# Low parts of x before the second norm, POOL for weight and constant splits, roots and scans in PSUM, and both projections on split parts

## The chip, the core and the metric
The kernel runs on one core of one Trainium2 chip. TensorE (PE) multiplies matrices into PSUM; VectorE (DVE), ScalarE (ACT) and GpSimd (POOL) work on tiles of 128 partitions; SyncE (SP) issues DMAs. Each engine works through its own queue in order, and semaphores tie the queues together. The metric is the device time of one execution in microseconds.

## The reference
The input x is 2 sequences of 512 tokens of 256 channels in float32. It is normalised, and the result xn goes through a gated linear recurrence and a ternary feed-forward network; both results are added to x:

```python
xn = layernorm(x)                                   # eps 1e-5, no scale
y = gelu(xn @ w_y + b_y)                            # exact gelu
xb = xn @ w_x + b_x
conv = conv_b + sum(conv_w[k] * shift(xb, 3 - k) for k in range(4))   # causal, per channel
gate_x, gate_a = sigmoid(conv @ w_ig + b_ig), sigmoid(conv @ w_ag + b_ag)
a = exp(-8 * gate_a * softplus(a_param));  mult = sqrt(1 - a * a)
a, mult = 0, 1 at t == 0
h[t] = a[t] * h[t-1] + gate_x[t] * conv[t] * mult[t]
attn = (h * y) @ w_out + b_out
q(w) = clip(round(w / mean|w|), -1, 1) * mean|w|    # hidden size 682
ffn = (silu(xn @ q(w1).T) * (xn @ q(w3).T)) @ q(w2).T
out = x + attn + ffn
```

## The kernel before, in words
Channels lie on partitions (2 chunks `c` of 128) and tokens along the free dimension, 512 for each sequence `s`. Nothing is scheduled by a planner: each engine has one hand-written list of steps, and the calls at its end set its order.

**Split products.** For a float32 product at the speed of fp32r matmuls a value is split into `hi` (a copy rounded to fp32r, mostly by ScalarE) and `lo` (value minus `hi`, by POOL or VectorE). A product is then three matmuls: w_hi with v_hi, w_lo with v_hi, w_hi with v_lo. The ternary weights are exact and need no low part. Only the projection with w_out (L706) multiplies plain float32.

**Stages.** TensorE keeps itself busy with products of ones (`warm`, L713). VectorE takes mean and variance of each token tile (L436, L441), POOL the root (L231, `pow`), VectorE normalises (L449). TensorE transposes (L636), ScalarE writes `xt_hi` (L288), VectorE `xt_lo` (L455). The product with w_x of sequence 0 (L740) works by halves of the sequence; `dense_terms` (L647) does all other products of the recurrent part. The newest tap of the convolution comes from ScalarE (L317), a correction of its first 3 columns (L488) and three older taps (L492) from VectorE. The gates follow (tanh, exp), then `squares` (a*a, L526). Ten tiles `n` = (s, j) of the hidden layer (L664) each pass through ScalarE's silu (L332), VectorE's product `g_of` (L514), ScalarE's `g_hi` (L338) and POOL's `g_lo` (L256); `silu` and `g` are rings of 3. A tail of 42 hidden units is handled by L673, L558, L566, L567 and L572. `down` (L696) sums the feed-forward output in PSUM.

**The end.** ScalarE takes four roots (`mult_of`, L370) after a table load. VectorE does for each of the four pairs (s, c) `gated_products` (L533), `scan` (L538) and `gated_output` (L544), all in SBUF, in place in `tx`. `project` adds w_out's product onto the same PSUM banks. VectorE adds x (L551), SP stores five pieces (L208).

## Time and profile before
| | |
|---|---|
| times of three runs | 75.23, 75.66, 76.0 us; median 75.66 |
| the profiled execution | 75.99 us, span 74.2 |
| granted TensorE clock | 1.0 of full speed |
| PE busy | 69.2 us, 93% of the span |
| DVE busy | 61.2 us, 82% |
| ACT busy | 48.3 us, 65% |
| POOL busy | 31.5 us, 43% |
| chain that ended last | PE 80%, DMA 7%, DVE 5%, SP's queue 3% |

Busy time of PE is that of matmuls that overlap, so it doesn't say that PE works at its peak. The chain is followed back from the last instruction to what released each one, so it shows where a saved microsecond counts. A row of the timeline gives the start, the duration, the engine and line, the tiles out<-in with their shapes, how many instructions are merged in it, and in brackets the idle time before it with what ended it. The duration of a row of several overlapping instructions is from the first start to the last end.

### The profile page before, as it was taken

The page shows a single profiled execution, that of the slowest core. Times are in us where ns is not written, and L with a number is a line of the kernel's source. Part 1 is how long each engine was busy: PE and PEld are TensorE (multiplying, and loading weights), DVE is VectorE, ACT ScalarE, POOL GpSimd, SP SyncE. Part 2 cuts the span into 40 slices and gives each one's busy share as a digit, 9 for nine tenths or more (in the row PEclk, how much of TensorE's full clock was granted, in tenths as well). Part 3 has the DMA queues.
Part 4 walks back from the last instruction along what each step waited for, and adds up shares of the span by engine and source line. Part 5 has one row for each costly group of instructions (what it writes and reads, how often), then busy time and mean ns, then how long its engine had stood idle before and what let it go on. Part 6 is the DMA issues. An engine that isn't in the chain of part 4 may idle for free.

```text
span 74.2 us, 1064 instructions
## 1 busy us (share of the span) xinstructions
PE 69.2 (93%) x364; PEld 58.6 (79%) x364; DVE 61.2 (82%) x101; ACT 48.3 (65%) x75; POOL 31.5 (43%) x43
## 2 busy tenths in 40 slices
PE   4999969999999999999999999999999999999920
PEld 4985758877888888888888888888899999988800
DVE  4897499999999999999979974697960799999750
ACT  3674523899999999999998978466699910000000
POOL 6385647245851680016002979947689000000000
PEclk9999999999999999999999999999999999999999
DMA  0889999920000000000000000000000000000195
GB/s 8 236 289 333 368 379 342 379 97 9 0 0 0 4 0 0 0 0 0 4 1 0 0 9 0 0 0 0 0 0 0 0 0 0 9 0 0 61 322 183
DMA packets 5095, 5.63 MB, mean 76 GB/s; under 512 B 525, under 2 KB 4578, under 8 KB 5090
## 3 DMA queue, kind: packets, MB, share of 16 engines
q1 hardware_dynamic: 4946, 5.55, 22.1%
q8 instruction: 3, 0.05, 0.3%
...
## 4 chain that ended last, share of the span: by engine, by line
PE 80%; DMA 7%; DVE 5%; SPq 3%; issue 1%; DVEq 0%
PE slot L664 25%; PE slot L647 23%; PE slot L696 14%; PE slot L706 8%; DMA x_sb<-x 7%; PE slot L767 4%; PE slot L673 2%; SPq L186 2%; DVE stats L436 2%; PE slot L740 2%; DVE x_sb L551 1%; PE slot L636 1%; DVE xt_lo L455 1%; SPq L183 1%; DVEq L52 0%
## 5 line engine op out<-in xcount | busy, mean ns | idle before, releaser
L256 POOL TENSOR_TENSOR g_lo<-w_raw,g_hi 128x512 fp32r<-128x512 f32 x10 | 14.1, 1421 | 9.0 <-ACT g_hi L338 8.9
L664 PE MATMUL slot<-xt_hi,w_q 128*128 128x512 f32 x40 | 15.7, 393 | 0.0
L664 PE MATMUL slot<-xt_lo,w_q 128*128 128x512 f32 x40 | 15.7, 393 | 0.0
L514 DVE SCALAR_TENSOR_TENSOR w_raw<-w_raw,s,slot 128x512 f32<-128x512 f32 x10 | 7.3, 747 | 3.1 <-ACT w_raw L332 3.0
L696 PE MATMUL slot<-w_q,g_hi 128*128 128x256 f32 x40 | 9.7, 283 | 0.0
L696 PE MATMUL slot<-w_q,g_lo 128*128 128x256 f32 x40 | 9.7, 283 | 0.0
L492 DVE SCALAR_TENSOR_TENSOR conv<-slot,par,conv 128x511 f32<-128x511 f32 (+2 forms) x12 | 9.0, 748 | 0.4
L664 PEld LDWEIGHTS slot<-xt_hi,w_q 128*128 128x128 f32 x40 | 7.5, 188 | 1.7
L664 PEld LDWEIGHTS slot<-xt_lo,w_q 128*128 128x128 f32 x40 | 7.5, 188 | 1.7
L332 ACT ACTIVATE w_raw<-slot,scale 128x512 f32<-128x512 f32 x10 | 6.6, 684 | 3.1 <-PE slot L664 3.1
L696 PEld LDWEIGHTS slot<-w_q,g_lo 128*128 128x128 f32 x40 | 7.7, 192 | 0.0
L696 PEld LDWEIGHTS slot<-w_q,g_hi 128*128 128x128 f32 x40 | 7.7, 192 | 0.0
L226 POOL TENSOR_TENSOR w_lo<-w_raw,w_hi 128x512 fp32r<-128x512 f32 x4 | 5.2, 1295 | 4.5 <-ACT w_hi L283 3.7
L706 PE MATMUL slot<-w_raw,tx 128*128 128x256 f32 x32 | 7.1, 379 | 0.0
L338 ACT ACTIVATE g_hi<-w_raw 128x512 fp32r<-128x512 f32 x10 | 6.3, 629 | 1.1 <-DVE w_raw L514 0.9
L251 POOL TENSOR_TENSOR conv_lo<-conv,conv_hi 128x512 fp32r<-128x512 f32 x4 | 5.4, 1354 | 3.3 <-ACT conv_hi L342 3.3
L706 PEld LDWEIGHTS slot<-w_raw,tx 128*128 128x128 f32 x32 | 6.0, 190 | 0.8
L713 PE MATMUL slot<-ones 128*128 128x128 f32 x28 | 5.3, 357 | 1.0 <-POOL ones L214 1.0
L713 PEld LDWEIGHTS slot<-ones 128*128 128x128 f32 x28 | 4.8, 261 | 1.4 <-POOL ones L214 1.0
L533 DVE TENSOR_TENSOR tx<-tx,mult 128x512 f32<-128x512 f32 x4 | 2.7, 685 | 2.8 <-ACT mult L370 2.8
L538 DVE TENSOR_TENSOR_SCAN tx<-ta,tx 128x512 f32<-128x512 f32 x4 | 4.9, 1224 | 0.1
L647 PE MATMUL slot<-conv_hi,w_hi 128*128 128x512 f32 x12 | 4.7, 395 | 0.0
...
## 6 DMA issues: line engine op xcount, KB each, us to landing
...
```

The lines of the kernel that those rows point to most:

```text
L226: nc.gpsimd.tensor_tensor(w_lo[:, m], w_raw[:, m], w_hi[:, m].bitcast(f32), ALU.subtract).then_inc(w_lo_set, 1)
L251: nc.gpsimd.tensor_tensor(conv_lo[:, s, c], conv[:, s, c], conv_hi[:, s, c].bitcast(f32), ALU.subtract).then_inc(conv_lo_set, 1)
L256: nc.gpsimd.tensor_tensor(g_lo[:, j, s], g[:, n % RING], g_hi[:, j, s].bitcast(f32), ALU.subtract).then_inc(g_lo_set, 1)
L332: nc.scalar.activation(silu[:, n % RING], slot[H_SLOT[s][j]][:, 0], ACT.Silu, scale=scale[:, 0:1]).then_inc(silu_set, 1)
L338: nc.scalar.activation(g_hi[:, j, s], g[:, n % RING], ACT.Copy).then_inc(g_hi_set, 1)
L492: nc.vector.scalar_tensor_tensor(out=conv[:, s, c, i:], in0=slot[X_SLOT[s]][:, c, 0:SEQ - i], scalar=par[:, CONV_W + KC * k + c:CONV_W + K ...
L514: nc.vector.scalar_tensor_tensor(out=g[:, n % RING], in0=silu[:, n % RING], scalar=s32[:, 0:1], in1=slot[H_SLOT[s][j]][:, 1], op0=ALU.mult ...
L647: mm = nc.tensor.matmul(dst[:, o], w[:, m, c, o * P:(o + 1) * P], v[:, c], start=(first and i == 0 and c == 0), stop=(last and i == len(te ...
L664: mm = nc.tensor.matmul(slot[H_SLOT[s][j]][:, o], w13_q[:, c, col:col + P], v[:, s, c], start=(c == 0 and v is xt_hi), stop=(c == KC - 1 a ...
L696: nc.tensor.matmul(out_tile(s, i, t), v[:, s, rows], w2_q[:, j], start=(j == 0 and t == tiles.start and k == 0), stop=False, skip_group_ch ...
L706: mm = nc.tensor.matmul(out_tile(s, i, t), tx[:, s, c, t * P:(t + 1) * P], w_raw[:, WOUT, c], start=False, stop=(c == KC - 1), skip_group_ ...
L713: nc.tensor.matmul(slot[WARM_SLOT][:, 0, 0:P], ones[:, :], ones[:, :], start=True, stop=True)
```

## The change
1. The low parts of x of sequence 0 come before the statistics of sequence 1 on VectorE, whose x is now loaded, measured and normalised in halves. TensorE does the product of half 0 with low parts before half 1.
2. POOL adds eps (L444 is gone), forms the constants of the taps behind the roots, makes w_hi of WIG, WAG and WOUT (a copy, `CAST`), w_lo of WY in two chunks behind the second norm, the decay rates, the padding of `gt` and the last `g_hi`.
3. The first 3 columns of the convolution are no longer corrected: `first_columns` writes them from PSUM with their own constants.
4. A gelu of one column early on ScalarE brings its table load forward.
5. The last silu stands behind g_hi(8). Roots are written to PSUM (`state`), in three banks that the hidden layer has left, and product and scan work there in place.
6. `gated_output` still writes `tx`. ScalarE copies it to `hy_hi`, POOL subtracts to `hy_lo` (the memory of `conv_hi` and `conv_lo`), and `project` uses three fp32r matmuls where there was one in float32. The fourth store is issued by ScalarE.

```diff
...
+        hy_hi, hy_lo = conv_hi, conv_lo
...
+        S_BANK = (slot[1][:, 1], slot[2][:, 0], slot[2][:, 1])
+        def state(s, c):
+            return S_BANK[(KC * s + c) % len(S_BANK)]
...
-            sp.dma_start(x_sb[:, 1], x_dram[1]).then_inc(x_loaded[TILES], 16)
+            for i in range(2):
+                t = slice(i * TILES // 2, (i + 1) * TILES // 2)
+                sp.dma_start(x_sb[:, 1, t], x_dram[1][:, t]).then_inc(x_loaded[TILES + i], 16)
...
-            for n, (s, i) in enumerate(O_ALL):
-                sp.wait_ge(o_set, n + 1)
-                t = slice(O_TILES[s][i].start, O_TILES[s][i].stop)
-                sp.dma_start(out_dram[s][:, t], x_sb[:, s, t]).then_inc(out_stored, 16)
+            for n in (0, 1, 2, 4):
+                store(sp, n)
...
+            def square_hi(m):
+                pool.wait_ge(w_loaded[m], 16)
+                nc.gpsimd.tensor_copy(w_hi[:, m], w_raw[:, m]).then_inc(w_hi_set, 1)
+            def square_lo(m, chunks=range(KC)):
                 pool.wait_ge(w_hi_set, m + 1)
-                nc.gpsimd.tensor_tensor(w_lo[:, m], w_raw[:, m], w_hi[:, m].bitcast(f32), ALU.subtract).then_inc(w_lo_set, 1)
+                c = slice(chunks.start, chunks.stop)
+                nc.gpsimd.tensor_tensor(w_lo[:, m, c], w_raw[:, m, c], w_hi[:, m, c].bitcast(f32), ALU.subtract).then_inc(w_lo_set, len(chunks))
...
+                pool.wait_ge(mv_set, TILES * s + tiles.stop)
+                nc.gpsimd.tensor_scalar(v_eps[:, s, tiles], mv[:, s, tiles, 1], EPS, None, ALU.add).then_inc(v_set, 1)
...
-            conv_constants()
-            nc.gpsimd.tensor_scalar(half_b[:, :], par[:, B_IG:B_IG + 2 * KC], 0.5, None, ALU.mult).then_inc(half_b_set, 1)
+            tap_biases()
+            tap_sum(0)
             rstd_of(0, slice(0, TILES // 2), 1)
             rstd_of(0, slice(TILES // 2, TILES), 2)
+            for i in range(1, TAPS):
+                tap_sum(i)
             pool.wait_ge(xn_set, TILES)
             square_lo(WX)
-            rstd_of(1, slice(0, TILES), 3)
-            square_lo(WY)
-            square_lo(WIG)
-            square_lo(WAG)
+            rstd_of(1, slice(0, TILES // 2), 3)
+            rstd_of(1, slice(TILES // 2, TILES), 4)
+            pool.wait_ge(xn_set, 2 * TILES)
+            for c in range(KC):
+                square_lo(WY, range(c, c + 1))
+            for m in (WIG, WAG):
+                square_hi(m)
+                square_lo(m)
+            lo_of_conv(0, 0)
+            half_biases()
+            rates()
+            lo_of_conv(0, 1)
+            gt_pads(slice(32, HALF), 1.0, KC)
+            pool.wait_ge(gt_pads_set, 1)
+            lo_of_conv(1, 0)
+            gt_pads(slice(96, P), 0.0, KC + 1)
+            pool.wait_ge(gt_pads_set, 2)
+            lo_of_conv(1, 1)
+            pool.wait_ge(a2_set, SEQS)
+            square_hi(WOUT)
+            square_lo(WOUT)
+            for n in range(2 * FULL):
+                if n == 2 * FULL - 1:
+                    pool.wait_ge(g_set, n + 1)
+                    nc.gpsimd.tensor_copy(g_hi[:, HJ[n][1], HJ[n][0]], g[:, n % RING]).then_inc(g_hi_set, 1)
+                lo_of_g(n)
+                if n == FULL - 1:
+                    pool.wait_ge(b_hi_set, 1)
+                    nc.gpsimd.tensor_tensor(b_split[:, 1], b_row[:, :], b_split[:, 0].bitcast(f32), ALU.subtract).then_inc(b_split_set, 1)
             for s in range(SEQS):
                 for c in range(KC):
-                    lo_of_conv(s, c)
-            pool.wait_ge(b_hi_set, 1)
-            nc.gpsimd.tensor_tensor(b_split[:, 1], b_row[:, :], b_split[:, 0].bitcast(f32), ALU.subtract).then_inc(b_split_set, 1)
-            for n in range(2 * FULL):
-                lo_of_g(n)
+                    pool.wait_ge(hy_hi_set, KC * s + c + 1)
+                    nc.gpsimd.tensor_tensor(hy_lo[:, s, c], tx[:, s, c], hy_hi[:, s, c].bitcast(f32), ALU.subtract).then_inc(hy_lo_set, 1)
...
+                act.wait_ge(mult0_set, KC * s + c + 1)
+                nc.scalar.activation(state(s, c)[:, 1:], mult[:, s, c, 1:], ACT.Sqrt, scale=-0.25, bias=quarter[:, 0:1]).then_inc(mult_set, 1)
+            def hy_hi_of(s, c):
+                act.wait_ge(hy_set, KC * s + c + 1)
+                act.wait_ge(ga_psum, s + 1)
+                nc.scalar.activation(hy_hi[:, s, c], tx[:, s, c], ACT.Copy).then_inc(hy_hi_set, 1)
...
             square_hi(WX)
+            act.wait_ge(quarter_set, 2)
+            nc.scalar.activation(gelu_in[:, 1:2], gelu_in[:, 0:1], ACT.Gelu)
             square_hi(WY)
             newest_tap(0)
-            square_hi(WIG)
             xt_hi_of(1)
...
+            for n in range(FULL, 2 * FULL - 1):
                 silu_of(n)
                 if n > FULL:
                     g_hi_of(n - 1)
-            g_hi_of(2 * FULL - 1)
-            for s in range(SEQS):
-                for c in range(KC):
-                    mult_of(s, c)
+            g_hi_of(2 * FULL - 2)
+            silu_of(2 * FULL - 1)
+            mult_of(0, 0)
+            mult_of(0, 1)
+            mult_of(1, 0)
+            hy_hi_of(0, 0)
+            mult_of(1, 1)
+            hy_hi_of(0, 1)
+            hy_hi_of(1, 0)
+            hy_hi_of(1, 1)
...
+            def first_columns(s, c):
+                dve.wait_ge(conv_c_set, TAPS)
+                dve.wait_ge(tap_set, KC * s + c + 1)
+                k = TAPS - 1
+                nc.vector.scalar_tensor_tensor(
+                    out=conv[:, s, c, 0:k], in0=slot[X_SLOT[s]][:, c, 0:k],
+                    scalar=par[:, CONV_W + KC * k + c:CONV_W + KC * k + c + 1],
+                    in1=conv_c[:, 0:k, c], op0=ALU.mult, op1=ALU.add).then_inc(tap_step, 1)
...
+            def first_root(s, c):
+                nc.vector.memset(state(s, c)[:, 0:1], 0.5).then_inc(mult0_set, 1)
...
-                nc.vector.tensor_tensor(tx[:, s, c], tx[:, s, c], mult[:, s, c], ALU.mult).then_inc(nx_set, 1)
+                nc.vector.tensor_tensor(state(s, c), tx[:, s, c], state(s, c), ALU.mult).then_inc(nx_set, 1)
...
-                nc.vector.tensor_tensor_scan(tx[:, s, c], ta[:, s, c], tx[:, s, c], 0.0, ALU.mult, ALU.add).then_inc(h_set, 1)
+                nc.vector.tensor_tensor_scan(state(s, c), ta[:, s, c], state(s, c), 0.0, ALU.mult, ALU.add).then_inc(h_set, 1)
...
-                nc.vector.tensor_tensor(tx[:, s, c], tx[:, s, c], y[:, s, c], ALU.mult).then_inc(hy_set, 1)
+                nc.vector.tensor_tensor(tx[:, s, c], state(s, c), y[:, s, c], ALU.mult).then_inc(hy_set, 1)
...
+            dense_terms(slot[Y_SLOT[0]], WY, [(w_hi, xt_hi[:, 0]), (w_hi, xt_lo[:, 0])], True, False)
+            transposes(1, first_half)
+            transposes(1, second_half)
+            pe.wait_ge(w_lo_set, KC * WY + 1)
+            dense_terms(slot[Y_SLOT[0]], WY, [(w_lo, xt_hi[:, 0])], False, True, chunks=[0])
+            pe.wait_ge(w_lo_set, KC * WY + 2)
+            dense_terms(slot[Y_SLOT[0]], WY, [(w_lo, xt_hi[:, 0])], False, True, chunks=[1]).then_inc(y_psum, 1)
...
```

(The order of TensorE's first products is shown below instead of its diff; that of the projection is this.)

```diff
...
-                pe.wait_ge(w_loaded[WOUT], 16)
+                pe.wait_ge(w_lo_set, KC * (WOUT + 1))
                 for c in range(KC):
-                    pe.wait_ge(hy_set, KC * s + c + 1)
-                    for i, tiles in enumerate(O_TILES[s]):
-                        for t in tiles:
-                            mm = nc.tensor.matmul(out_tile(s, i, t), tx[:, s, c, t * P:(t + 1) * P], w_raw[:, WOUT, c],
-                                                  start=False, stop=(c == KC - 1), skip_group_check=True)
-                        if c == KC - 1:
-                            mm.then_inc(o_psum, 1)
-            def warm(count):
+                    for k, (v, w, ready) in enumerate(((hy_hi, w_hi, hy_hi_set), (hy_hi, w_lo, hy_hi_set), (hy_lo, w_hi, hy_lo_set))):
+                        pe.wait_ge(ready, KC * s + c + 1)
+                        for i, tiles in enumerate(O_TILES[s]):
+                            for t in tiles:
+                                mm = nc.tensor.matmul(out_tile(s, i, t), v[:, s, c, t * P:(t + 1) * P], w[:, WOUT, c],
+                                                      start=False, stop=(c == KC - 1 and k == 2), skip_group_check=True)
+                            if c == KC - 1 and k == 2:
+                                mm.then_inc(o_psum, 1)
...
```

TensorE's first products. `xt_hi` and `xt_lo` are the split x, `w_hi` and `w_lo` the split weights; 128x256 are half a sequence of w_x's product, 128x512 a whole sequence of w_y's. Before:

```order
L636 MATMUL slot<-ident,xn_y 128x128 x8
L740 MATMUL slot<-xt_hi,w_hi 128x256 x8
L740 MATMUL slot<-xt_hi,w_lo 128x256 x8
L740 MATMUL slot<-xt_lo,w_hi 128x256 x8
L647 MATMUL slot<-xt_hi,w_hi 128x512 x4
L647 MATMUL slot<-xt_hi,w_lo 128x512 x4
L636 MATMUL slot<-ident,xn_y 128x128 x8
L647 MATMUL slot<-xt_lo,w_hi 128x512 x4
```

After (the four pairs of xt_hi and xt_lo of 128x512 are shown once):

```order
L725 MATMUL slot<-ident,xn_y 128x128 x4
L803 MATMUL slot<-ones 128x64
L725 MATMUL slot<-ident,xn_y 128x128 x4
L828 MATMUL slot<-xt_hi,w_hi 128x256 x4
L828 MATMUL slot<-xt_lo,w_hi 128x256 x4
L828 MATMUL slot<-xt_hi,w_hi 128x256 x4
L828 MATMUL slot<-xt_hi,w_lo 128x256 x8
L828 MATMUL slot<-xt_lo,w_hi 128x256 x4
L736 MATMUL slot<-xt_hi,w_hi 128x512
L736 MATMUL slot<-xt_lo,w_hi 128x512
...
L725 MATMUL slot<-ident,xn_y 128x128 x8
L736 MATMUL slot<-xt_hi,w_lo 128x512 x4
```

Half 0 gets its low parts before half 1 gets its high parts, and the matmuls with w_lo of w_y moved behind the transposes of sequence 1.

POOL between its first root and the first low part of the convolution. Before:

```order
L259 TENSOR_SCALAR half_b<-par 128x4
L231 TENSOR_TENSOR rstd<-v_eps,power 128x2 x2
L226 TENSOR_TENSOR w_lo<-w_raw,w_hi 128x512
L231 TENSOR_TENSOR rstd<-v_eps,power 128x4
L226 TENSOR_TENSOR w_lo<-w_raw,w_hi 128x512 x3
L251 TENSOR_TENSOR conv_lo<-conv,conv_hi 128x512 x4
```

After:

```order
L246 TENSOR_TENSOR w_lo<-w_raw,w_hi 128x512
L259 TENSOR_SCALAR v_eps<-mv 128x2
L262 TENSOR_TENSOR rstd<-v_eps,power 128x2
L259 TENSOR_SCALAR v_eps<-mv 128x2
L262 TENSOR_TENSOR rstd<-v_eps,power 128x2
L246 TENSOR_TENSOR w_lo<-w_raw,w_hi 128x256 x2
L241 CAST w_hi<-w_raw 128x512
L246 TENSOR_TENSOR w_lo<-w_raw,w_hi 128x512
L241 CAST w_hi<-w_raw 128x512
L246 TENSOR_TENSOR w_lo<-w_raw,w_hi 128x512
L289 TENSOR_TENSOR conv_lo<-conv,conv_hi 128x512
```

The w_lo of w_y went into two halves behind both roots, and two copies stand before the low parts of the gates' weights.

ScalarE's end. `w_raw<-slot,scale` is silu, `g_hi<-w_raw` the high part of g. Before:

```order
L332 ACTIVATE w_raw<-slot,scale 128x512
L338 ACTIVATE g_hi<-w_raw 128x512 x2
L370 ACT_TABLE_LOAD
L370 ACTIVATE mult<-mult,quarter 128x511 x4
L52 UNCONDITIONAL_BRANCH
```

After:

```order
L400 ACTIVATE g_hi<-w_raw 128x512 x2
L394 ACTIVATE w_raw<-slot,scale 128x512
L433 ACT_TABLE_LOAD
L433 ACTIVATE slot<-mult,quarter 128x511 x3
L439 ACTIVATE conv_hi<-tx 128x512
L433 ACTIVATE slot<-mult,quarter 128x511
L439 ACTIVATE conv_hi<-tx 128x512 x3
L190 DMA out<-x_sb 128x256
```

The last silu moved behind g_hi(8), g_hi(9) left the engine, and the four copies to `hy_hi` (shown by their memory, conv_hi) are new.

## Rows read from the trace of the kernel before

**Rows 1.** The chain that ended last, one piece: start, us, what.
```profile
53.53 10.56 PE slot L696 x88
```

**Rows 2.** TensorE's timeline: start us, us, engine line, out<-in, count, idle before.
```profile
10.90 1.34 PE L740 MATMUL slot<-xt_lo,w_hi 128*128 128x256 f32 x8 [0.63 <-DVE xt_lo L455]
12.08 1.08 PE L647 MATMUL slot<-xt_hi,w_hi 128*128 128x512 f32 x4
...
13.91 1.04 PE L636 MATMUL slot<-ident,xn_y 128*128 128x128 f32 x8
...
15.71 0.47 PE L647 MATMUL slot<-xt_hi,w_hi 128*128 128x512 f32 x1
...
33.05 0.39 PE L664 MATMUL slot<-xt_hi,w_q 128*128 128x512 f32 x1
...
63.92 7.07 PE L706 MATMUL slot<-w_raw,tx 128*128 128x256 f32 x32
```

**Rows 3.** VectorE's timeline at the start, with the first norm tile alone.
```profile
8.37 1.41 DVE L436 BATCH_NORM_STATS2 stats<-x_sb 128x6 f32<-128x256 f32 x4 [0.97 <-DMA x_sb<-x]
9.69 0.36 DVE L441 BATCH_NORM_AGGREGATE mv<-stats 128x2 f32<-128x6 f32 x4
...
11.38 2.34 DVE L449 TENSOR_SCALAR xn_y<-x_sb,mv,rstd 128x256 f32<-128x256 f32 x4
...
11.38 1.37 DVE L449 TENSOR_SCALAR xn_y<-x_sb,mv,rstd 128x256 f32<-128x256 f32 x1
```

**Rows 4.** VectorE's timeline, the ternary weights in the middle.
```profile
28.19 3.22 DVE L471 SCALAR_TENSOR_TENSOR w_q<-w_raw,thr,below 128x1408 fp32r<-128x1408 f32 x2
```

**Rows 5.** VectorE's timeline, the first and last of the end.
```profile
57.87 0.69 DVE L533 TENSOR_TENSOR tx<-tx,mult 128x512 f32<-128x512 f32 x1 [2.83 <-ACT mult L370]
...
67.89 0.69 DVE L544 TENSOR_TENSOR tx<-tx,xn_y 128x512 f32<-128x512 f32 x1
...
70.17 1.35 DVE L551 TENSOR_TENSOR x_sb<-slot,x_sb 128x512 f32<-128x512 f32 x3 [0.39 <-PE slot L706]
```

**Rows 6.** POOL's timeline at the start.
```profile
1.07 0.31 POOL L217 MEMSET w_raw<- 128x256 f32 x1
...
4.91 0.22 POOL L259 TENSOR_SCALAR half_b<-par 128x4 f32<-128x4 f32 x1
5.09 1.53 POOL L231 TENSOR_TENSOR rstd<-v_eps,power 128x2 f32<-128x2 f32 x2
...
11.31 1.29 POOL L226 TENSOR_TENSOR w_lo<-w_raw,w_hi 128x512 fp32r<-128x512 f32 x1
```

**Rows 7.** Groups by line and shape: busy us, mean ns, idle before.
```profile
L492 DVE SCALAR_TENSOR_TENSOR conv<-slot,par,conv 128x511 f32<-128x511 f32 x4 | 3.0, 749 | 0.1
L455 DVE TENSOR_TENSOR xt_lo<-slot,xt_hi 128x512 fp32r<-128x512 f32 x4 | 2.6, 680 | 0.0
L520 DVE SCALAR_TENSOR_TENSOR tx<-tx,conv 128x1024 f32<-128x1024 f32 x2 | 2.4, 1215 | 0.0
...
L471 DVE SCALAR_TENSOR_TENSOR w_q<-w_raw,thr,below 128x1408 fp32r<-128x1408 f32 x1 | 1.7, 1672 | 0.0
...
L338 ACT ACTIVATE g_hi<-w_raw 128x512 fp32r<-128x512 f32 x10 | 6.3, 629 | 1.1 <-DVE w_raw L514 0.9
...
L256 POOL TENSOR_TENSOR g_lo<-w_raw,g_hi 128x512 fp32r<-128x512 f32 x10 | 14.1, 1421 | 9.0 <-ACT g_hi L338 8.9
```

**Rows 8.** ScalarE's timeline at the end.
```profile
53.57 0.69 ACT L332 ACTIVATE w_raw<-slot,scale 128x512 f32<-128x512 f32 x1 [0.64 <-PE slot L664]
54.34 1.37 ACT L338 ACTIVATE g_hi<-w_raw 128x512 fp32r<-128x512 f32 x2
55.72 1.28 ACT L370 ACT_TABLE_LOAD   x1
57.02 2.56 ACT L370 ACTIVATE mult<-mult,quarter 128x511 f32<-128x511 f32 x4
```

**Rows 9.** The stores of line 208: ns min/median/max, first and last issue.
```profile
L208 SPq DMA_DIRECT2D out<-x_sb x5: 372/428/499, 69.2 to 71.8; - x5
```

More of the change, by code:

```diff
@@ L401, in _ @@
             decays(1)
-            act.wait_ge(w_lo_set, WIG + 1)
+            act.wait_ge(w_lo_set, KC * (WIG + 1))
             silu_of(0)
@@ L441, in variance @@
                     nc.vector.bn_aggr(mv[:, s, t], stats[:, s, t]).then_inc(mv_set, 1)
-                dve.wait_ge(mv_set, TILES * s + tiles.stop)
-                t = slice(tiles.start, tiles.stop)
-                nc.vector.tensor_scalar(v_eps[:, s, t], mv[:, s, t, 1], EPS, None, ALU.add).then_inc(v_set, 1)
             def normalise(s, tiles, ready):
@@ L630, in _, with transposes @@
         def _(pe):
-            def transposes(s):
-                for t in range(TILES):
+            def transposes(s, tiles):
+                for t in tiles:
                     pe.wait_ge(xn_set, TILES * s + t + 1)
@@ L639, in transposes, with dense_terms @@
                         mm.then_inc(xt_psum, 1)
-            def dense_terms(dst, m, terms, first, last, chunk_ready=None):
-                for c in range(KC):
+            def dense_terms(dst, m, terms, first, last, chunk_ready=None, chunks=range(KC)):
+                for c in chunks:
                     if chunk_ready:
@@ L732, in sum_of_w2, with first_x_terms @@
                 nc.tensor.matmul(sum2, ones[:, :], abs_sum[:, 2:4], start=True, stop=True).then_inc(sum2_psum, 1)
-            def first_x_terms(weights, part, ready):
-                for h in range(2):
-                    pe.wait_ge(ready, h + 1)
-                    for c in range(KC):
-                        for o in range(KC):
-                            for w in weights:
-                                mm = nc.tensor.matmul(slot[X_SLOT[0]][:, o, halves[h]], w[:, WX, c, o * P:(o + 1) * P],
-                                                      part[:, 0, c, halves[h]],
-                                                      start=(part is xt_hi and h == 0 and c == 0 and w is w_hi),
-                                                      stop=(part is xt_lo and c == KC - 1), skip_group_check=True)
+            def first_x_terms(weights, part, ready, h):
+                pe.wait_ge(ready, h + 1)
+                for c in range(KC):
+                    for o in range(KC):
+                        for w in weights:
+                            mm = nc.tensor.matmul(slot[X_SLOT[0]][:, o, halves[h]], w[:, WX, c, o * P:(o + 1) * P],
+                                                  part[:, 0, c, halves[h]],
+                                                  start=(part is xt_hi and h == 0 and c == 0 and w is w_hi),
+                                                  stop=(part is xt_lo and h == 1 and c == KC - 1), skip_group_check=True)
@@ L755, in _ @@
-            transposes(1)
-            dense_terms(slot[Y_SLOT[0]], WY, [(w_hi, xt_lo[:, 0])], False, True).then_inc(y_psum, 1)
+            first_x_terms((w_hi,), xt_hi, xt_hi_set, 0)
+            first_x_terms((w_hi,), xt_lo, xt_lo_set, 0)
+            first_x_terms((w_hi,), xt_hi, xt_hi_set, 1)
+            pe.wait_ge(w_lo_set, KC * (WX + 1))
+            for h in range(2):
+                first_x_terms((w_lo,), xt_hi, xt_hi_set, h)
+            first_x_terms((w_hi,), xt_lo, xt_lo_set, 1).then_inc(xb_psum, 1)
@@ L778, in _ @@
             sums_of_w13()
-            pe.wait_ge(w_lo_set, WAG + 1)
+            pe.wait_ge(w_lo_set, KC * (WAG + 1))
             for o in range(KC):
```

127 lines of the change are left out of this document (67 added, 60 removed).

## The prediction
> **What bounds the kernel now.** I read the chain of waits first, then each engine's timeline at the two ends of the kernel, where that chain leaves TensorE, and in the middle.
>
> The chain runs through TensorE from 10.90 us to the end of its last matmul; one of its pieces is the down projection, 88 matmuls in 10.56 us, 0.12 each [rows 1]. The projection behind it shows 32 rows in 7.07 us, two rows for one fp32 matmul: 16 matmuls at 0.44 [rows 2]. Yet other chains run close behind:
> - at the start TensorE sits idle for 0.63 us until VectorE has the low parts of x (10.90), and its second transposes, at 13.91, come just after VectorE's second norm, which ends at 13.72 [rows 2, 3];
> - in the middle VectorE ends the ternary weights at 31.41 and TensorE uses them at 33.05, 1.6 us of room [rows 2, 4];
> - at the end VectorE's chain of product, scan and product, 57.87 to 68.58 [rows 5], delivers its last tile 0.6 us before TensorE, busy with its own queue, gets to it (8 rows of 0.22 before 70.99, so 69.2 [rows 2]).
>
> **Start: what TensorE gains.** VectorE loses two fills, the two steps on the rates and three on v_eps. POOL gets v_eps, and no longer stands in constants (until 4.91 + 0.22) before its two roots, 5.09 to 6.62 [rows 6]. I estimate them 0.45 and 0.2 earlier, and so the norm of sequence 0 ends at about 7.2. From there I lay out the new order with the old durations. Half 0: high parts on ScalarE (0.60) until 7.28, low parts on VectorE (0.68 [rows 7]) until 8.0. TensorE: 4 products of 0.12, a short wait, 4 with low parts at 8.07, 4 high ones of half 1 at 8.55, 8 with w_lo (POOL, 1.29 [rows 6], ready at 8.6) at 9.03, the last 4 from 10.0 to 10.48. Before, the next product followed at 12.08 [rows 2]: 1.5 us earlier.
>
> **Start: what is late next.** VectorE now takes the statistics of sequence 1 behind the low parts: from 9.1, four statistics in 1.41 and four variances in 0.36 [rows 3], with hand-overs, so its halves are ready at 10.15 and 11.15. POOL needs 0.22 for v_eps and 0.78 for a root [rows 6]: roots at 11.25 and 12.3. Four tiles took 2.34, 1.37 of it the first alone, because it collided with POOL's w_lo, 11.31 to 12.60 [rows 3, 6]; the other three took 0.33 each. Now w_lo of WY stands behind the whole norm, which ends, with a 3-column tap in between, at about 13.1. Then POOL takes w_lo in two halves of 256 columns. None was timed; with a fixed part of at most 0.2 (the 4-column row) in the 1.29 I take 0.74, so 13.15 to 14.55; bounds 0.65 and 1.29 each. TensorE has done Y's 8 products (0.23 each, from 10.6) at 12.45, transposes until 13.6, idles for a while, and does the last four with w_lo until 15.1. Before, the product of sequence 1 started at 15.71 [rows 2]. **Gain 0.6 us**, not 1.5; bounds 0 (long halves) and 1.5 (nothing is late).
>
> At no cost: gelu's table load (1.28), moved to 8.4, between the high parts and w_hi of WY, which comes at 10.5, when TensorE asks for it; x in halves, since the whole had landed at 8.37 [rows 3] and is wanted at 9.1; the one more DMA issue on SP (0.4), behind which weights stand that are used microseconds later. If one of these covers failed, it would cost its delay, at most 0.5.
>
> **Middle: nothing.** VectorE's taps start 0.8 us earlier, so thresholds and ternary weights keep their room. POOL takes both high parts of WIG and WAG. No row has a POOL copy; bounds 0.31 (a fill of 256 columns) and 1.29 (the subtraction) [rows 6]. I take 0.8, the middle, since it reads one input where the subtraction reads two. Then conv_lo of (0,1) is there at 22.2, needed at 23.0; at 1.29 it is 0.4 late. The high and low part of WOUT on POOL come before g_lo(0), which is wanted only by the fourth g.
> By the Trainium skill ("GPSIMD Engine Reference", § 3.1) the best loop would take 768 ns for 512 elements, which no run here shows.
>
> **End: when the roots can start.** Before: two g_hi (54.34, 1.37), the table load at 55.72, the first root at 57.02 [rows 8]. After, at an unchanged hidden layer: g_hi(8) until 54.97, the last silu (0.69) behind it until 55.57, the load until 56.87; POOL takes g_hi(9). That is **0.15 earlier**, and with the 0.6 VectorE's chain starts at 57.12 instead of 57.87.
>
> **End: the chain itself.** It lasts 10.71, plus one memset and its wait, 0.1. Roots, products and scans now lie in PSUM. No row has a VectorE write to PSUM, but reads do: a subtraction from PSUM takes 680 ns, a product of SBUF alone 0.69 us [rows 5, 7]; a scalar_tensor_tensor of 511 columns from PSUM 749 and one of 1408 from SBUF 1672, which is 1.03 ns a column between them, so that neither memory is dearer [rows 7]. I take **zero**.
> By the Trainium skill ("VectorE: DVE Perf Modes", § The TRN2 errata) the fixed part is 58 cycles from SBUF and 120 from PSUM; the twelve instructions would by that cost an estimated 0.78 us more.
>
> **End: the new hand-over.** Before, from the end of the last hy (68.58) to the first output that waited (70.17): 1.59 [rows 5]. After: ScalarE copy 0.63 [rows 7], POOL subtraction 1.29 (bound above 1.42, the mean of g_lo [rows 7]), two matmuls and their tail 0.5, four waits of 0.05: 2.62. So **+1.03**. POOL's subtraction doesn't hold up VectorE: each of the twelve has one SBUF input now, like the taps, which kept their 749. The projection has 48 matmuls at 0.12, 5.8 us instead of 7.07, but this is no gain: all that it shortens lies beside VectorE's chain. The last store was issued at 71.8 behind another on SP's queue, 0.3 after its tile (71.52) [rows 5, 9]; with its neighbour moved to ScalarE's queue it follows at once: **-0.27**.
>
> **Sum.** -0.6 - 0.15 + 0.1 + 1.03 - 0.27 = +0.1 us. The profiled execution took 75.99, the median of the runs shown is 75.66: 76.1 by the one, **75.8** by the other.
>
> **Rivals.**
> 1. The forecast, 0.50: 75.2 to 76.4 with the smaller bounds.
> 2. The whole early lead stays, 0.24. For: POOL's pieces are small there, and the low-part products fill TensorE's wait. Against: the norm hangs on POOL's roots. Then -1.5 in place of -0.6, 74.9; with writes to PSUM cheaper by 0.03 on twelve instructions 74.5.
> 3. PSUM operands cost VectorE more, 0.17. Place: the twelve instructions from the first root to the last hy. Price: the 1024-column scalar_tensor_tensor in SBUF took 1215, which scales to 687 at 511 columns, against 749 from PSUM [rows 7]. If that 0.06 is the memory's, and not that of the pointer that only the tap has, the path grows by 0.72: 76.5. It makes the kernel slower from 0.05 an instruction on; the 1408-column row, which has a pointer too, speaks against it.
> The Trainium skill's "VectorE: DVE Perf Modes" stands on this side with its 62 cycles.
> 4. The lead is lost, 0.09: POOL late with w_lo or conv_lo. 76.2 to 76.8.
> That the change doesn't do what it says is excluded by the order of its instructions.
>
> About 1% is what a measurement tells here: below 74.9 faster, above 76.4 slower. Faster: 0.22 of rival 2 and 0.05 of the forecast, 0.27. Slower: 0.15 of rival 3, 0.05 of rival 4, 0.07 of the forecast, 0.27. Same: 0.46. Range 74.6 to 76.9: nearly all of rival 2, and rival 3 with some 0.4 of the other bounds on top.
>
> **What the new profile would show.** Right: TensorE idles about 1 us in all between 12.5 and 14.6; the first product of sequence 1 near 15.1; the first root at about 56.3; products 0.69 and scans 1.22; at the end the chain is VectorE, ScalarE's copy, POOL's subtraction, four matmuls, outputs. Wrong: no idle TensorE there (rival 2); products at 0.74 and more (rival 3); a wait of TensorE for POOL between 15 and 24 us (rival 4). If at 70 us TensorE is busy up to its last matmul, instead of waiting for POOL, my end is wrong.

## The result, and the profile after it
The changed kernel takes **76.81 us** (median of 4 runs, 76.70 to 76.91); the kernel before took 75.58 on the same chip (4 runs, 75.23 to 76.00). The ratio is 1.019, 95% interval 1.014 to 1.024: 1.9% slower, where I had forecast no change. (In the jobs of the experiments some executions of the kernel before were over 1.5% above its fastest; ratios leave them out.) Its profiled execution took 76.88 us with a span of 75.1, against 75.99 and 74.2: so 0.9 us are to be found in the traces.

PE is now busy 68.3 us (91%), DVE 60.2 (80%), ACT 49.3 (66%), POOL 45.3 (60%; it was 31.5). The chain that ended last has left TensorE, whose share fell from 80% to 38%. One line of the page gives its shares by engine:

```profile
PE 38%; DVE 23%; issue 12%; POOL 10%; ACT 7%; DMA 3%; POOLq 2%; DVEq 1%; ACTq 0%
```

**The start went as planned.** TensorE's timeline, to be read against [rows 2]:

```profile
12.66 1.03 PE L725 MATMUL slot<-ident,xn_y 128*128 128x128 f32 x8
13.93 1.43 PE L736 MATMUL slot<-xt_hi,w_lo 128*128 128x512 f32 x4 [0.23 <-POOL w_lo L246]
15.20 0.40 PE L736 MATMUL slot<-xt_hi,w_hi 128*128 128x512 f32 x1
...
32.26 0.39 PE L753 MATMUL slot<-xt_hi,w_q 128*128 128x512 f32 x1
...
53.45 0.28 PE L785 MATMUL slot<-w_q,g_hi 128*128 128x256 f32 x1
```

The first product of sequence 1 starts at 15.20 instead of 15.71, 0.5 us earlier, behind POOL's two short w_lo. At the first hidden tile the lead is 0.8: 32.26 against 33.05. The row of 53.45, the first of the down projection, is for later.

**The end.** VectorE's timeline from the first root on, to be read against [rows 5]:

```profile
57.49 0.70 DVE L614 TENSOR_TENSOR slot<-tx,slot 128x512 f32<-128x512 f32 x1 [1.18 <-ACT slot L433]
58.23 1.23 DVE L619 TENSOR_TENSOR_SCAN slot<-ta,slot 128x512 f32<-128x512 f32 x1
...
60.32 0.06 DVE L608 MEMSET slot<- 128x1 f32 x1
...
67.75 0.69 DVE L625 TENSOR_TENSOR tx<-slot,xn_y 128x512 f32<-128x512 f32 x1
68.36 1.28 DVE L632 TENSOR_TENSOR x_sb<-slot,x_sb 128x512 f32<-128x512 f32 x2
71.07 1.36 DVE L632 TENSOR_TENSOR x_sb<-slot,x_sb 128x512 f32<-128x512 f32 x3 [1.43 <-PE slot L796]
```

The last hy is done at 68.44, earlier than before (68.58), and yet the outputs that waited start at 71.07 instead of 70.17. What lies between stands on three engines, here in order of time (from the timelines of ScalarE, POOL and TensorE):

```profile
68.48 0.63 ACT L439 ACTIVATE conv_hi<-tx 128x512 fp32r<-128x512 f32 x1 [2.03 <-DVE tx L625]
69.19 1.29 POOL L336 TENSOR_TENSOR conv_lo<-tx,conv_hi 128x512 fp32r<-128x512 f32 x1 [1.38 <-ACT conv_hi L439]
70.53 0.74 PE L796 MATMUL slot<-w_hi,conv_lo 128*128 128x256 f32 x4
```

Copy, subtraction, matmuls: the first output waits for two of the last four. Span by span: the chain starts 0.38 earlier (57.87 to 57.49), lasts 0.24 longer (10.95), the hand-over costs 1.04 more (2.63): +0.90, which is the whole difference of the two profiled executions. The medians lie 1.2 apart; run 6 below shows where the rest may come from.

**Where the lead went.** It was 0.8 at the first hidden tile, and at the projection nothing is left: TensorE comes to it at 63.99 (before 63.92). VectorE had used up its own room before that. VectorE's timeline:

```profile
24.30 2.74 DVE L539 TENSOR_SCALAR below<-w_raw,thr 128x1408 bf16<-128x1408 f32 x2
26.96 4.26 DVE L542 SCALAR_TENSOR_TENSOR w_q<-w_raw,thr,below 128x1408 fp32r<-128x1408 f32 x2
...
39.11 1.98 DVE L598 SCALAR_TENSOR_TENSOR tx<-tx,conv 128x1024 f32<-128x1024 f32 x1
...
47.56 0.71 DVE L647 CAST gt_hi<-w_raw 42x1024 fp32r<-42x1024 f32 x1
48.30 2.37 DVE L648 CAST gt<-w_raw 42x1024 fp32r<-42x1024 f32 x1
50.71 1.41 DVE L592 SCALAR_TENSOR_TENSOR w_raw<-w_raw,s,slot 128x512 f32<-128x512 f32 x2
```

and POOL's beside it:

```profile
24.72 1.59 POOL L285 MEMSET gt<- 32x1024 f32 x1
26.39 1.79 POOL L289 TENSOR_TENSOR conv_lo<-conv,conv_hi 128x512 fp32r<-128x512 f32 x1
...
38.70 1.30 POOL L246 TENSOR_TENSOR w_lo<-w_raw,w_hi 128x512 fp32r<-128x512 f32 x1
39.95 3.55 POOL L294 TENSOR_TENSOR g_lo<-w_raw,g_hi 128x512 fp32r<-128x512 f32 x2
...
47.68 1.19 POOL L332 TENSOR_TENSOR b_split<-b_row,b_split 1x256 fp32r<-1x256 f32 x1
48.84 1.29 POOL L294 TENSOR_TENSOR g_lo<-w_raw,g_hi 128x512 fp32r<-128x512 f32 x1
```

Each of these VectorE rows, but for the first cast and the last row, lies beside POOL rows that are new or were elsewhere before. The same instructions in the kernel before, on VectorE:

```profile
25.11 3.16 DVE L468 TENSOR_SCALAR below<-w_raw,thr 128x1408 bf16<-128x1408 f32 x2
...
40.14 1.22 DVE L520 SCALAR_TENSOR_TENSOR tx<-tx,conv 128x1024 f32<-128x1024 f32 x1
...
48.74 0.69 DVE L567 CAST gt<-w_raw 42x1024 fp32r<-42x1024 f32 x1
...
51.37 2.15 DVE L572 TENSOR_TENSOR gt<-w_raw,gt_hi 42x1024 fp32r<-42x1024 f32 x1
```

The ternary weights took 6.3 us (25.11 to 31.41, [rows 4]) and now take 6.9, so their lead shrinks from 0.8 to 0.2; the gated input grows by 0.76. The cast is the worst, 1.7 longer. Its own POOL neighbour, b_split, ends at 48.87 and g_lo behind it at 50.13; the cast ends at 50.67, 0.54 behind g_lo. By these times it has waited for both. It holds up the product behind it, and TensorE waits for that.

```profile
51.51 0.50 PE L753 MATMUL slot<-xt_hi,w_q 128*128 128x512 f32 x1 [0.61 <-DVE w_raw L592]
```

These 0.61 are its only wait in the hidden layer. Counted from row to row it loses 0.9: this tile, the last, started at 51.52 before, the down projection at 53.37. Here is that row of the kernel before:

```profile
53.37 0.28 PE L696 MATMUL slot<-w_q,g_hi 128*128 128x256 f32 x1
```

So from its first tile to the down projection the hidden layer takes 21.2 us (32.26 to 53.45), where it took 20.3 (33.05 to 53.37). What counts is not how many collisions there are, but what stands behind them: the kernel before has one too, its subtraction of the tail, which took 2.15 at 51.37 beside a g_lo and takes 1.22 now. But two products of the ring stood ahead of it (49.46 and 50.59), and TensorE waited for nothing.

### The profile page after: what moved, and what is told of

It is laid out like the page before. It is cut to its first block, busy times and chain, and to the rows that moved or that the text cites. A ratio compares the mean times of both kernels' runs of the same rounds, so it can differ in the third digit from the quotient of the medians.

```text
span 75.1 us, 1125 instructions
## 1 busy us (share of the span) xinstructions
PE 68.3 (91%) x378; PEld 58.6 (78%) x378; DVE 60.2 (80%) x98; ACT 49.3 (66%) x77; POOL 45.3 (60%) x62
## 4 chain that ended last, share of the span: by engine, by line
PE 38%; DVE 23%; issue 12%; POOL 10%; ACT 7%; DMA 3%; POOLq 2%; DVEq 1%; ACTq 0%
PE slot L736 20%; PE slot L753 10%; DVE slot L619 5%; DVE w_raw L592 5%; PE slot L860 4%; POOL rstd L262 4%; ACT w_raw L394 3%; DMA par<-params 3%; DVE slot L614 3%; POOL w_lo L246 3%; DVE gt L648 3%; PE slot L762 2%; DVE xn_y L520 2%; DVE tx L625 2%; POOLq L52 2%
## 5 line engine op out<-in xcount | busy, mean ns | idle before, releaser
L294 POOL TENSOR_TENSOR g_lo<-w_raw,g_hi 128x512 fp32r<-128x512 f32 x10 | 14.8, 1497 | 2.6 <-ACT g_hi L400 2.5
L336 POOL TENSOR_TENSOR conv_lo<-tx,conv_hi 128x512 fp32r<-128x512 f32 x4 | 5.2, 1290 | 6.4 <-ACT conv_hi L439 6.4
L400 ACT ACTIVATE g_hi<-w_raw 128x512 fp32r<-128x512 f32 x9 | 5.7, 629 | 4.7 <-DVE w_raw L592 4.7
L241 POOL CAST w_hi<-w_raw 128x512 fp32r<-128x512 f32 x3 | 1.8, 611 | 9.8 <-DVE mult L604 9.8
L246 POOL TENSOR_TENSOR w_lo<-w_raw,w_hi 128x512 fp32r<-128x512 f32 (+1 forms) x6 | 6.6, 1112 | 1.4 <-DVE xn_y L520 0.9
L439 ACT ACTIVATE conv_hi<-tx 128x512 fp32r<-128x512 f32 x4 | 2.5, 632 | 7.4 <-DVE tx L625 7.4
L803 PE MATMUL slot<-ones 128*128 128x128 f32 (+1 forms) x26 | 5.3, 385 | 1.0 <-POOL ones L229 1.0
L510 DVE BATCH_NORM_STATS2 stats<-x_sb 128x6 f32<-128x256 f32 x8 | 3.1, 418 | 2.5 <-DMA x_sb<-x 2.5
L619 DVE TENSOR_TENSOR_SCAN slot<-ta,slot 128x512 f32<-128x512 f32 x4 | 4.9, 1229 | 0.1
```

The source lines that it names most:

```text
L246: nc.gpsimd.tensor_tensor(w_lo[:, m, c], w_raw[:, m, c], w_hi[:, m, c].bitcast(f32), ALU.subtract).then_inc(w_lo_set, len(chunks))
L294: nc.gpsimd.tensor_tensor(g_lo[:, j, s], g[:, n % RING], g_hi[:, j, s].bitcast(f32), ALU.subtract).then_inc(g_lo_set, 1)
L400: nc.scalar.activation(g_hi[:, j, s], g[:, n % RING], ACT.Copy).then_inc(g_hi_set, 1)
L619: nc.vector.tensor_tensor_scan(state(s, c), ta[:, s, c], state(s, c), 0.0, ALU.mult, ALU.add).then_inc(h_set, 1)
L803: nc.tensor.matmul(slot[WARM_SLOT][:, 0, 0:cols], ones[:, :], ones[:, 0:cols], start=True, stop=True)
```

## Experiments
My theory after the two traces was in two parts: (A) the new hand-over costs 1.0 us and the shorter projection gives nothing back, and (C) the lead is lost to collisions of POOL's moved pieces with VectorE. The rival: the time is lost on TensorE, or in VectorE's chain of roots, products and scans. Runs 1 to 4 went together, then 5, 6, 7 and 11, last 8 to 10; each job timed the kernel before as well (medians 75.5, 75.3 and 75.6 us of the executions that count), and ratios are against that. The three jobs ran on three chips, so a difference between runs of two jobs, or against the changed kernel, is good to some tenths only. The texts on record call a run by its label: fp32_proj (1), bias_early (2), both (3), fp32_last (4), moved_pool (5), split_alone (6), sbuf_states (7), pool_silu (8), pool_last (9), pool_fp32 (10), best (11).

**1. The changed kernel, projection in float32 again.**

```diff
-                        for k, (v, w, ready) in enumerate(((hy_hi, w_hi, hy_hi_set), (hy_hi, w_lo, hy_hi_set), (hy_lo, w_hi, hy_lo_set))):
+                        for k, (v, w, ready) in enumerate(((tx, w_raw, hy_set),)):
```

> The changed kernel with its projection back in one float32 product (16 matmuls from tx and the raw w_out; no hy_hi, no hy_lo); roots and scans stay in PSUM, POOL's split of w_out stays. Theory A (the new hand-over through ScalarE and POOL costs what the sum said, 1.03 us): outputs start at about 70.2 as before the change, 0.9 us less than the changed kernel, so about 75.9. Rival B (PSUM operands or VectorE's later chain set the end, the hand-over is hidden): no change, 76.8.

Measured 76.00 us, ratio 1.007 (1.004 to 1.011): 0.8 less than the changed kernel. The outputs that wait start at 70.09, and wait for TensorE's own queue only. So the split of the projection costs 0.8 net at this place.

```profile
70.09 1.36 DVE L624 TENSOR_TENSOR x_sb<-slot,x_sb 128x512 f32<-128x512 f32 x3 [0.60 <-PE slot L791]
```

**2. The changed kernel, only the split of b_out put back to where it was** (behind the last conv_lo on POOL, its high part behind `decays(0)` on ScalarE).

```diff
             lo_of_conv(1, 1)
+            pool.wait_ge(b_hi_set, 1)
+            nc.gpsimd.tensor_tensor(b_split[:, 1], b_row[:, :], b_split[:, 0].bitcast(f32), ALU.subtract).then_inc(b_split_set, 1)
```

> The changed kernel with the split of b_out where it was before (ScalarE behind the first decays, POOL behind conv_lo), else unchanged. In the changed kernel VectorE's second cast of the tail took 2.37 us instead of 0.69, beside POOL's b_split and g_lo(5) back to back, and TensorE idled 0.6 us behind it. Theory C (that pair held the cast up and ate TensorE's early lead): cast back to about 0.7, no idle of TensorE in the hidden layer, roots 0.4 to 0.5 earlier, about 76.35. Rival D (g_lo(5) alone holds it up as long, or the silu chain is late for another reason): 76.7 to 76.8, cast still over 1.5 us.

Measured 77.06 us, 1.022 (1.013 to 1.031): **the expectation fell**. The cast is short again, as expected, but the 256 elements now meet another small step (VectorE, then POOL):

```profile
31.61 0.68 DVE L551 TENSOR_TENSOR s<-scale 128x1 f32<-128x1 f32 x1
```
```profile
31.54 0.72 POOL L323 TENSOR_TENSOR b_split<-b_row,b_split 1x256 fp32r<-1x256 f32 x1 [3.28 <-ACT b_split L466]
```

0.68 instead of 0.14, and all behind it is later. Then the gated input meets POOL's w_lo of w_out (39.64 to 40.94):

```profile
39.71 2.32 DVE L597 SCALAR_TENSOR_TENSOR tx<-tx,conv 128x1024 f32<-128x1024 f32 x1
```

It took 1.98 in the changed kernel. The third product of the ring starts at 43.38 instead of 42.44, and TensorE waits for it at 44.18 (0.65). A collision taken away in one place came up in two others, and the hidden layer still takes 21.2 us.

**3. Both edits at once.**

> Both edits together. If A and C are right and independent, TensorE keeps its early lead of about 0.6 us to the end and is the bound again: about 75.0, faster than the kernel before by 0.6. If only A is right, 75.9; if only C, 76.35.

Measured 76.22 us, 1.010 (1.006 to 1.013): 1.2 above what I expected. TensorE idles 0.66 at 43.60 as in run 2, and the hidden layer takes 21.2 us. The b_out split alone is not the cause of the lost lead.

**4. Run 2, with the last pair (1,1) alone projected in float32.**

```diff
+                    terms = ((tx, w_raw, hy_set),) if (s, c) == (SEQS - 1, KC - 1) else split
```

> Split of b_out early, and the projection on split parts for three of the four pairs, but the last pair (1,1) in float32 from tx, so that nothing stands between VectorE's last product and TensorE but a semaphore. Theory A: TensorE has the first three done at about 67.8, VectorE gives the last at about 68.0, two float32 matmuls and their tail take 1.2, outputs start at about 69.2: 74.7. Rival (TensorE, not the hand-over, is the bound at the end): equal to both edits together, about 75.0 or more.

Measured 76.12 us, 1.006 (1.003 to 1.010): 0.94 less than run 2, and 1.4 above what I expected. As a size of the hand-over 0.94 is right (1.03 on record); the level is off because the lead is lost here too. It is no better than float32 for all four pairs (run 3, 76.22). No output waits for anything any more:

```profile
68.72 2.66 DVE L630 TENSOR_TENSOR x_sb<-slot,x_sb 128x512 f32<-128x512 f32 x5
```

**5. The changed kernel, all of POOL's movable pieces moved.** The padding of `gt` is filled by VectorE at its start, b_out is split before the two conv_lo of sequence 1, and w_out behind the last g_lo (its high part by ScalarE behind the third root).

```diff
-            gt_pads(slice(32, HALF), 1.0, KC)
-            gt_pads(slice(96, P), 0.0, KC + 1)
-            square_hi(WOUT)
-            square_lo(WOUT)
...
             for n in range(2 * FULL):
                 lo_of_g(n)
+            square_lo(WOUT)
```

> The changed kernel with POOL's new work moved out of VectorE's way and nothing else: the padding of gt is filled by VectorE at its start, where it waits 2 us for x; b_out is split at about 17.5 us (ScalarE) and 22.3 (POOL); w_out is split at the end (ScalarE behind its third root, POOL behind the last g_lo). Theory C2 (POOL pieces beside VectorE's ternary weights, its gated input and its tail casts use up TensorE's early lead of 0.6 us): the four ternary instructions take 6.3 us again and not 7.0, no cast over 1 us, no idle of TensorE in the hidden layer, the first root 0.4 to 0.5 earlier, 76.3. Rival D (the lead ends in the ring of silu and g, whatever POOL does): TensorE still idles 0.6, 76.8.

Measured 76.08 us, 1.010 (1.006 to 1.014): 0.73 less than the changed kernel, with the same arithmetic. VectorE's timeline:

```profile
24.27 1.79 DVE L535 TENSOR_SCALAR below<-w_raw,thr 128x1408 bf16<-128x1408 f32 x2
25.97 4.28 DVE L538 SCALAR_TENSOR_TENSOR w_q<-w_raw,thr,below 128x1408 fp32r<-128x1408 f32 x2
...
38.52 1.22 DVE L594 SCALAR_TENSOR_TENSOR tx<-tx,conv 128x1024 f32<-128x1024 f32 x1
...
47.91 0.69 DVE L644 CAST gt<-w_raw 42x1024 fp32r<-42x1024 f32 x1
...
50.55 2.15 DVE L649 TENSOR_TENSOR gt<-w_raw,gt_hi 42x1024 fp32r<-42x1024 f32 x1
...
56.83 0.70 DVE L610 TENSOR_TENSOR slot<-tx,slot 128x512 f32<-128x512 f32 x1 [1.18 <-ACT slot L426]
```

Cast and gated input have their old lengths, `below` went from 2.74 to 1.79, TensorE has no wait in the hidden layer, comes to the projection at 63.10 instead of 63.99, and the chain starts at 56.83 instead of 57.49. The lead of the start reaches the end, and that settles (C) for these pieces together; which of them costs how much is not kept apart. Two collisions are left, w_q beside a conv_lo of 1.68 and the subtraction of the tail (2.15, as before the change), and neither makes TensorE wait.

A count that doesn't depend on when an execution gets going says the same of all kernels: from its first row to the down projection the hidden layer takes 21.19 to 21.25 us in the changed kernel and in runs 1, 2, 3, 4 and 7, and 20.31 to 20.32 in the kernel before and in runs 5, 6, 8, 9, 10 and 11.

**6. The kernel before, with the split projection alone**, roots and scans in SBUF as before.

> The kernel before with one thing added: the projection on split parts (w_out split by ScalarE behind the roots and by POOL behind the last g_lo, hy_hi by ScalarE, hy_lo by POOL); roots and scans stay in SBUF. Theory A: the hand-over costs 1.0 us by itself, so at least 76.6. Theory P (each product and scan has two SBUF inputs and collides with POOL's hy_lo): VectorE's chain from the first product to the last hy grows from 10.7 to 11.5 or more, 77.3 to 78.5. Rival (no collision): chain 10.7, 76.6.

Measured 81.03 us, 1.076 (1.058 to 1.093): theory P, but 2.5 above its upper end. The chain takes 14.4 us instead of 10.7, and the hand-over 2.63 instead of 1.59; these two make about 4.7 us of the difference.

Up to the roots this is the code of the kernel before, so its trace shows that code a second time (VectorE, TensorE, VectorE):

```profile
8.06 1.41 DVE L449 BATCH_NORM_STATS2 stats<-x_sb 128x6 f32<-128x256 f32 x4 [0.65 <-DMA x_sb<-x]
```
```profile
32.74 0.39 PE L677 MATMUL slot<-xt_hi,w_q 128*128 128x512 f32 x1
```
```profile
57.56 0.69 DVE L546 TENSOR_TENSOR tx<-tx,mult 128x512 f32<-128x512 f32 x1 [2.83 <-ACT mult L377]
```

All three lie 0.31 earlier than in the first trace (8.37, 33.05 and 57.87): there x of sequence 1 landed later, and the statistics, which TensorE's low parts stand behind, wait for it in both. Against this trace the changed kernel leads by 0.5 at the first hidden tile, not 0.8, and its chain starts 0.07 earlier, not 0.38. The spans then add up to +1.2, as the medians do. Which of the two is the rule, two traces don't show.

**7. The changed kernel with roots, products and scans in SBUF.**

```diff
-                nc.vector.tensor_tensor(state(s, c), tx[:, s, c], state(s, c), ALU.mult).then_inc(nx_set, 1)
+                nc.vector.tensor_tensor(tx[:, s, c], tx[:, s, c], mult[:, s, c], ALU.mult).then_inc(nx_set, 1)
```

> The changed kernel with roots, products and scans back in SBUF (mult and tx), projection still on split parts. Theory P: PSUM does nothing for the duration of one instruction (692 against 685 ns, scans 1,229 against 1,224), but keeps VectorE clear of POOL's hy_lo; without it the chain grows from 10.95 us by 0.5 to 2, so 77.3 to 78.8. Rival (PSUM is neutral beside POOL too): 76.7, the 0.2 of the memset between the pairs saved and nothing lost.

Measured 80.18 us, 1.062 (1.050 to 1.075): 3.4 us above the changed kernel, more than the 0.5 to 2.0 that I had allowed. Run 7's VectorE, and its POOL, in the same stretch:

```profile
58.13 2.20 DVE L620 TENSOR_TENSOR_SCAN tx<-ta,tx 128x512 f32<-128x512 f32 x1
...
63.09 1.54 DVE L626 TENSOR_TENSOR tx<-tx,xn_y 128x512 f32<-128x512 f32 x1
...
68.73 1.22 DVE L620 TENSOR_TENSOR_SCAN tx<-ta,tx 128x512 f32<-128x512 f32 x1
70.06 1.50 DVE L626 TENSOR_TENSOR tx<-tx,xn_y 128x512 f32<-128x512 f32 x1
```
```profile
68.84 2.18 POOL L336 TENSOR_TENSOR conv_lo<-tx,conv_hi 128x512 fp32r<-128x512 f32 x1 [1.29 <-ACT conv_hi L439]
```

The chain lasts 14.2 us instead of 10.95 (14.4 in run 6). These rows also show what the two engines do to each other. The product of 70.06 ends at 71.56; POOL's subtraction beside it ran from 68.84 for 2.18, to 71.02. It had itself begun 0.11 behind a scan (68.73, 1.22) and ends 1.07 behind that scan's end, where alone it takes 1.29; the product ends 0.54 behind the subtraction, where alone it takes 0.69. The times fit if each waits for the whole of the other that came first. So PSUM is worth nothing for one instruction alone (below), and 3.3 us for twelve of them beside POOL's subtractions. The two halves of the change belong together.

**8. Run 5, with the last silu and the first root ahead of g_hi(8).** (The text on record speaks of two roots; the edit moves one.)

```diff
-            g_hi_of(2 * FULL - 2)
             silu_of(2 * FULL - 1)
             mult_of(0, 0)
+            g_hi_of(2 * FULL - 2)
```

> moved_pool with one more edit: the last silu and the first two roots stand ahead of g_hi(8) on ScalarE, all four pairs keep the split projection. Theory A (VectorE's chain and the hand-over behind it are the only bound): the chain starts 1.0 us earlier than moved_pool's 56.83, the hand-over stays 2.6, 75.1 us. Theory B (g_hi(8) late delays the down projection, and TensorE then delays the end): first root earlier, but TensorE idles behind the hidden layer and the gain is under 0.4, 75.7 or more.

Measured 75.03 us, 0.991 (0.987 to 0.995). The chain starts at 55.53, 1.3 earlier than in run 5. Its first hidden tile was 0.3 earlier already (31.95 against 32.23), so 1.0 is the edit's, as expected. The hand-over of 2.6 ends last (last hy 66.47):

```profile
69.09 1.35 DVE L628 TENSOR_TENSOR x_sb<-slot,x_sb 128x512 f32<-128x512 f32 x3 [1.43 <-PE slot L792]
```

**9. Run 5, with the last pair in float32.**

> moved_pool with one more edit: the last pair (1,1) is projected in plain float32, so no ScalarE copy and no POOL subtraction stand behind the last tile of VectorE's chain. By the hand-over (2.63 with the split, about 1.6 without, of which TensorE needs 8 rows of 0.22 behind its queue): 75.2 us, 0.9 less than moved_pool's 76.08. If TensorE's own queue ends last instead (down projection, then three split pairs): 75.7.

Measured 74.91 us, 0.991 (0.987 to 0.995): 1.2 less than run 5, where I had expected 0.9. The five outputs follow the chain without a wait, from 67.73.

**10. Run 5 with the silu order of run 8, all four pairs in float32.**

> moved_pool with the last silu ahead of g_hi(8), and all four pairs projected in plain float32 (no parts of w_out or of hy at all). TensorE then has 7.07 us of projection behind its down projection instead of 5.8. Theory A (only VectorE's chain counts): as best, 74.3. Theory B (the split pays for TensorE once the chain starts early): TensorE's queue ends last, from a start at about 63.3 the outputs come at 69.6 instead of best's 68.45, and the time is 75.3.

Measured 74.92 us, 0.992 (0.989 to 0.995). Theory B of that text holds, though 0.4 below its time: the last hy is done at 66.45, but TensorE is busy with its own queue. A row of TensorE and one of VectorE:

```profile
62.81 7.07 PE L785 MATMUL slot<-w_raw,tx 128*128 128x256 f32 x32
```
```profile
69.06 1.35 DVE L618 TENSOR_TENSOR x_sb<-slot,x_sb 128x512 f32<-128x512 f32 x3 [1.41 <-PE slot L785]
```

**11. Both edits, 8 and 9**: POOL's pieces moved, three pairs split, the last in float32, silu and first root ahead of g_hi(8).

> POOL's work moved as in the kernel of that name; the last silu ahead of g_hi(8), so that the table load and the first root come 0.6 us earlier (load at about 54.0, root at 55.3); the last pair of the projection in float32, the other three split. Theories A and C2 together: VectorE gives the last hy at 66.9, TensorE has the other three pairs done at 67.7 and is the bound again, outputs start at about 69.0, so about 74.5, 1.1 under the kernel before. If TensorE's lead is lost in the hidden layer anyway: 75.1. If the roots don't come earlier: 75.0.

Measured **74.31 us** (74.27 to 74.34, 4 runs), 0.984 (0.974 to 0.993): faster than both kernels, by the ratio 1.2 below the one before, and 2.5 below the changed one's median. ScalarE's table load moved from 55.41 in the changed kernel to 53.73, and the outputs wait 0.49 for TensorE, whose last four float32 matmuls (eight rows) begin without a gap.

```profile
53.73 1.28 ACT L426 ACT_TABLE_LOAD   x1 [0.28 <-DVE slot L603]
```
```profile
68.45 1.35 DVE L627 TENSOR_TENSOR x_sb<-slot,x_sb 128x512 f32<-128x512 f32 x3 [0.49 <-PE slot L794]
```

Runs 8, 10 and 11 stand side by side: with the early chain, the outputs that wait start at 69.09 with all split, by the hand-over, at 69.06 with none, by TensorE's queue, and at 68.45 with three of four, though in run 11 the hidden layer began 0.3 later than in the other two (32.24 against 31.95 and 31.94).

## Why the prediction was wrong
**Start, gain 0.6: right** in place and nearly in size (0.51 at the product of sequence 1, 0.79 at the hidden layer; against the trace of run 6, 0.23 and 0.48). The terms ahead of it were nearly all right too: roots of 0.71 and 0.73 at 10.57 and 11.56, w_lo of WY from 13.14 in 1.43, the first product of sequence 1 at 15.20 (15.1 on record). Only the norm of sequence 0 came no earlier than before (7.45 instead of 7.2), and TensorE idled 0.23 and not 1 us.

**"Middle: nothing": this step failed**, and with it the -0.6 of the sum. The middle costs 0.9 us (hidden layer 21.2 instead of 20.3). I asked of each of POOL's new pieces only whether POOL would be late, priced its copy (0.8; it took 0.61), and left out what it does to VectorE, though [rows 3, 6] had shown just that at 11.38: a norm tile of 1.37 where the next ones took 0.33, beside w_lo. I had even used that row, for another place. Two fills and the split of b_out were not priced at all; they are small, but the cast beside b_split and the g_lo behind it took 2.37. Run 5 gives the lead back by moving these pieces and nothing else (-0.73). The Trainium skill has this rule in "SBUF — State Buffer", § Who interferes with whom: a VectorE instruction with two SBUF inputs and one of POOL's that reads SBUF, or a VectorE copy, cast or tensor_scalar in a two-port mode and any of POOL's, take one pair of ports by turns, and the second waits for the whole of the first. The trace agrees: the cast ended 0.54 behind g_lo. Read against POOL's new list, it would have named this step before the result.

**Rival 4 is the one that came, by another mechanism.** Its time (76.2 to 76.8) ends where the result lies, but I put the loss on TensorE waiting for POOL between 15 and 24 us. TensorE waited for POOL only at 13.9, for 0.23; the loss is on VectorE from 24 to 51 us. Its chance of 0.09 was too low: a lead won at the start has to pass 35 us in which any POOL piece may meet VectorE.

**Chain start, 0.15 earlier: right.** ScalarE's rows:

```profile
54.18 0.63 ACT L400 ACTIVATE g_hi<-w_raw 128x512 fp32r<-128x512 f32 x1 [0.96 <-DVE w_raw L592]
54.72 0.67 ACT L394 ACTIVATE w_raw<-slot,scale 128x512 f32<-128x512 f32 x1
55.41 1.28 ACT L433 ACT_TABLE_LOAD   x1
```

From g_hi(8) to the table load 1.23 us pass, where 1.38 passed ([rows 8], 54.34 to 55.72): 0.15 less. The chain starts 0.38 earlier in all, 0.16 of it since g_hi(8) itself does; in the trace of run 6 g_hi(8) starts at 54.03, and of that nothing is left.

**Chain of product and scan: right.** Its length is 10.95 (10.81 expected). Products take 0.69, scans 1.23 and roots 0.68 in PSUM, where they took 0.69, 1.22 and 0.71 in SBUF, so rival 3 is false. By the Trainium skill ("VectorE: DVE Perf Modes", § The TRN2 errata) PSUM's fixed part is 62 cycles dearer, by its figures an estimated 0.065 us. The rows here don't bear that out (means of 692 ns against 685 for the product with the root, 1,229 against 1,224 for the scan), and the measurement decides. The memset between the first two pairs cost 0.2 instead of 0.1: the next product starts at 60.37, 0.12 behind the end of the one ahead, where at a later pair it starts 0.08 before that end.

**"POOL's subtraction doesn't hold up VectorE": right**, and runs 6 and 7 show its condition and its worth. I gave it one sentence; it is the largest effect in this case, 3.3 us.

**Hand-over, +1.03: right.** 2.63 measured, 2.62 on record. Runs 1 and 4 take away 0.8 and 0.94 us of the time. That TensorE's shorter projection is no gain was right as well; it becomes one only once the chain starts at 55.5 (runs 10 and 11).

**Last store, -0.27: half right.** It is issued right behind its tile, at 72.46, but from there to the end 2.6 us pass, where it was 2.4 before. From the last tile's end to the end of the span it is 2.7 us in both, so the term is worth nothing; why the rest grew stays open.

The sum with measured terms: -0.38 + 0.24 + 1.04 = +0.90 of span, and nothing of the store, instead of -0.75 + 0.1 + 1.03 - 0.27 = +0.1 on record. Of the 0.8 between them 0.37 is what is missing at the chain's start, which is the lost lead, 0.27 the store, 0.14 the chain. The medians lie 1.2 apart and the two profiled executions 0.9. Against the trace of run 6 the missing start is 0.68, and the terms make the whole 1.2. So the forecast also leaned on an execution that lost 0.3 us more than another in a wait for x (0.97 in [rows 3]). The change takes that wait off VectorE's path (its statistics of sequence 1 start at 9.22 and wait for nothing), so part of the gain that the rows promised may not have been there to be had on the median of 75.66; two traces don't prove it.
